# Routed expert rows in grains of 256: two experts' odd grains share one of 20 jobs per half

## What is computed

```python
def _moe_forward(x, Wfc_s, bfc_s, Wproj_s, bproj_s, Wr, Wfc, bfc, Wproj, bproj):
    shared = new_gelu(xf @ Wfc_s + bfc_s) @ Wproj_s + bproj_s        # 128 -> 512 -> 128
    topk_p, topk_i = jax.lax.top_k(jax.nn.softmax(xf @ Wr), 2)
    ...                                                              # gate: the two, normalised
    for e in range(8):
        h = new_gelu(xf @ Wfc[e] + bfc[e]) @ Wproj[e] + bproj[e]
        routed = routed + h * gate[:, e:e + 1]
    return shared + routed
...
x = x + 0.5 * _L0_ffn_ref(_layernorm(x), ...)
x = x + _L0_attn_ref(_layernorm(x), ...)
x = x + 0.5 * _L0_ffn_ref(_layernorm(x), ...)
```

## Time and profile before

| | us |
|---|---|
| median of 3 runs | 1620.02 (1619.47 to 1620.25) |
| the profiled execution's own time | 1619.65 |
| its span, first to last instruction | 1617.8 |
| mean granted clock of TensorE | 0.933 of full |
| PE busy in the span | 87% |
| DVE, ACT, POOL busy | 70%, 63%, 58% |

### The profile page before, as it was taken

The page is one execution under the profiler, slowest core; times in us unless marked ns, Lnnn a source line. Parts: engine busy times, 40 slices in busy tenths (PEclk is TensorE's granted clock), DMA queues, the critical chain, the costliest instruction groups (busy, mean ns, idle before and its releaser), DMA issues.

```text
span 1617.8 us, 31349 instructions
## 1 busy us (share of the span) xinstructions
PE 1414.1 (87%) x10792; PEld 1102.2 (68%) x10792; DVE 1136.0 (70%) x2292; ACT 1017.4 (63%) x1765; POOL 942.4 (58%) x742
## 2 busy tenths in 40 slices
PE   5689899999996799999999999677999999999700
PEld 4668788888884566666666666576877888887500
DVE  7767666667884688888777777576776666788522
ACT  3145478888884477777777777313556888878600
POOL 3168888405661388888565555534877850377176
PEclk9999999999998699999999999758999999999955
DMA  9801256556662646445444443000115655566522
GB/s 264 266 33 42 85 185 201 167 167 192 197 200 91 188 149 174 150 147 170 135 135 142 137 143 106 9 1 23 41 44 189 210 180 157 180 199 199 150 78 74
DMA packets 244702, 226.53 MB, mean 140 GB/s; under 512 B 31809, under 2 KB 188737, under 8 KB 244545
## 3 DMA queue, kind: packets, MB, share of 16 engines
q1 hardware_dynamic: 179584, 166.83, 32.6%
q0 software_dynamic: 16384, 33.59, 7.5%
q10 hardware_dynamic: 48576, 24.12, 5.0%
HBM read 85.34 MB, written 90.70 MB: 109 GB/s over the span
## 4 chain that ended last, share of the span: by engine, by line
PE 40%; issue 9%; POOL 7%; ACT 5%; DVE 4%; DMA 1%; POOLq 0%; DVEq 0%; ACTq 0%; SPq 0%
PE psum L851 5%; POOL x_slots L652 5%; PE psum L832 5%; PE psum L866 3%; PE psum L313 3%; ACT ret_absed L1001 2%; PE psum L315 2%; PE psum L314 2%; PE psum L296 2%; PE psum L295 2%; PE psum L294 2%; PE psum L906 2%; POOL ring L663 2%; PE psum L239 2%; DVE ret_f L1115 1%
## 5 line engine op out<-in xcount | busy, mean ns | idle before, releaser
L663 POOL DMA_INDIRECT ring<-y_slots,slot x256 | 279.1, 1090 | 303.6 <-DMA y_slots<-ffn_y_rows 198.1
L652 POOL DMA_INDIRECT x_slots<-ffn_xn,slot x256 | 323.5, 1263 | 147.5 <-issue 77.4
L598 DVE TENSOR_TENSOR ffn_h_lo<-ffn_h,ffn_h_hi 128x1024 fp32r<-128x1024 f32 x248 | 304.0, 1226 | 8.6
L385 ACT ACTIVATE ffn_h<-psum,ffn_bias_up 128x512 f32<-128x512 f32 x368 | 236.4, 682 | 6.0
L588 DVE TENSOR_TENSOR ffn_x_lo<-psum,ffn_x_hi 128x512 fp32r<-128x512 f32 x124 | 85.8, 692 | 205.6 <-ACT ffn_x_hi L367 205.4
L1261 POOL TENSOR_TENSOR ret_ssum<-ret_ssum,ret_power 128x32 f32<-128x32 f32 x32 | 174.4, 5449 | 42.5 <-DVE ret_ssum L1169 42.3
L1145 DVE TENSOR_TENSOR ret_masked<-psum,ret_mask 128x512 f32<-128x512 f32 x256 | 174.8, 683 | 23.4 <-PE psum L832 18.5
L1001 ACT ACTIVATE ret_absed<-ret_masked 128x1536 f32<-128x1536 f32 x128 | 190.1, 1485 | 1.5 <-PE psum L866 0.4
L596 DVE CAST ffn_h_hi<-ffn_h 128x1024 fp32r<-128x1024 f32 x248 | 171.2, 690 | 7.7 <-PE psum L315 7.5
L995 ACT ACTIVATE ret_masked<-psum 128x256 f32<-128x256 f32 x256 | 96.9, 380 | 105.4 <-DVE ret_masked L1145 105.0
L313 PE MATMUL psum<-ffn_h_hi,ffn_w_down 128*128 128x512 f32 x368 | 152.3, 414 | 5.9 <-issue 5.5
(11 more groups left out here) (155 smaller groups left out, 3059.7 us busy)
## 6 DMA issues: line engine op xcount, KB each, us to landing
qk_copies<-ret_parts SPq DMA_DIRECT2D x128, 256.0 KB
ret_qk<-qk_copies SPq DMA_DIRECT2D x32, 1024.0 KB, 5.6
ffn_xj<-x_slots SPq DMA_DIRECT2D x92, 256.0 KB
ffn_w_up<-w_hi SPq DMA_DIRECT2D x92, 256.0 KB
ffn_w_up<-w_lo SPq DMA_DIRECT2D x92, 256.0 KB
y_slots<-ffn_y_rows ACTq DMA_DIRECT2D x92, 256.0 KB, 3.3
x_slots<-ffn_y_rows SPq DMA_DIRECT2D x46, 256.0 KB, 3.5
x_slots<-ffn_xn,slot POOLq DMA_INDIRECT x256, 2.7
```

Of the source, the lines that this page charges most:

```text
L385: act.activation(h[2 * (n % 2) + c // 2][:, (c % 2) * JOB:(c % 2 + 1) * JOB], up_ps[c % UP_RING], ACT.Gelu_apprx_tanh, bias=bias[:, c:c + ...
L598: dve.tensor_tensor(h_lo[s][:], buf[:], h_hi[s][:].bitcast(F32), ALU.subtract).then_inc(lo_done, 1)
L652: pool.indirect_dma_start(m["x_slot_rows"][half], slots_of(half, k), xn[:, half * HALF + k // 2, :], None)\
L663: pool.indirect_dma_start(ring[:, k % G_RING, :], None, m["y_slot_rows"][half], slots_of(half, k % BLOCKS))\
```

## The change

The unit that an expert's rows are rounded up to is now a grain of 256 rows, `GRAIN`. An expert with an odd number of grains in a half puts its odd grain into a pair job, where it shares 512 rows with the odd grain of another expert; all other grains go in twos into whole jobs, as before. A half has 32 grains and at most 7 more by rounding, so 20 jobs: 4 pair jobs and 16 whole ones. A layer has 16 + 40 = 56 jobs.

- **A pair job** has two weight sets. Its up and down matmuls go by columns 0 to 255 with the first set and 256 to 511 with the second: 24 up and 24 down matmuls of 256 columns. Each gelu and the reading of `y` are split in two (`shares`). `up` waits for both sets before its first matmul.
- **Up weights.** `w_up` still has two buffers, now one per set. SP waits, before set s, for the gelus of the job that used set s-2. A pair uses both buffers.
- **Down weights.** `w_down` has two buffers too; `down_schedule` puts each set's copy at the earliest hidden stage at which its buffer is free. `w_down1` lies over constants that routing alone uses, so the copies wait for `slots_done`.
- **Order.** 13 shared jobs; then pair, shared, pair, shared, pair, shared, pair of the first half; its 16 whole jobs; then the second half, as pair and three whole jobs four times over, and four whole ones.
- **Routing.** `place` on DVE has more steps, 19 more increments of `route` per layer.

```diff
+GRAIN = JOB // 2
-HALF_JOBS = MOST + NE - 1
+PAIR_JOBS = NE // 2
+HALF_JOBS = -(-(TOKENS // GRAIN + NE - 1) // 2)
-SHARED_FIRST = 16
+SHARED_FIRST = 13
...
+    order = shared[:SHARED_FIRST] + pairs[0][:1]
+    for pair, between in zip(pairs[0][1:], shared[SHARED_FIRST:]):
+        order += [between, pair]
+    order += whole[0]
+    for i, pair in enumerate(pairs[1]):
+        order += [pair] + whole[1][3 * i:3 * i + 3]
+    order += whole[1][3 * PAIR_JOBS:]
...
+def down_schedule(jobs):
+    users, slots, last = set_users(jobs), {}, -1
+    for s, (job, i) in sorted(users.items()):
+        free = users[s - 2][0]["n"] + 2 if s >= 2 else 0
+        at = min(max(job["n"], free, last + (i > 0)), job["n"] + 1)
+        assert at >= free
+        slots.setdefault(at, []).append(s)
+        last = at
+    return slots
...
     def place_up(sp, job):
+        for at, s in enumerate(job["sets"]):
+            e = sp.value_load(table[0:1, job["entry"] + at:job["entry"] + at + 1], min_val=1, max_val=NE)
+            if s >= 2:
+                sp.wait_ge(gelu_done, CH * (users[s - 2][0]["n"] + 1))
...
         def up(job):
+            for s in job["sets"]:
+                pe.wait_ge(up_ready[s % 2], up_weights_at(s))
...
+                for cols, parts in zip(shares(job), weights):
+                    bank = up_ps[c % UP_RING][:, cols]
...
+                for cols, added in zip(shares(job), bias):
+                    last = act.activation(to[:, cols], up_ps[c % UP_RING][:, cols], ACT.Gelu_apprx_tanh, bias=added[:, c:c + 1])
...
+            for cols, of in halves_of:
+                dve.tensor_tensor(beyond[:, :, cols], position[:, :, cols], whole_slots[:, of].unsqueeze(2).to_broadcast(wide),
+                                  ALU.is_ge).then_inc(route, 1)
...
+            for cols, of in halves_of:
+                dve.tensor_tensor(beyond[:, :, cols], beyond[:, :, cols], shift[:, of].unsqueeze(2).to_broadcast(wide), ALU.mult)\
+            dve.tensor_tensor(slot_part, slot_part, beyond, ALU.add).then_inc(route, 1)
```

More of the change, by code:

```diff
@@ L67, in job_order @@
-    return jobs
+    pairs, whole = ([[("routed", HALF_JOBS * half + k) for k in ks] for half in range(2)]
+                    for ks in (range(PAIR_JOBS), range(PAIR_JOBS, HALF_JOBS)))
+    order = shared[:SHARED_FIRST] + pairs[0][:1]
[5 more added lines that the diff above has]
+    order += whole[1][3 * PAIR_JOBS:]
+    assert sorted(order) == sorted(shared + pairs[0] + whole[0] + pairs[1] + whole[1])
@@ new lines, in job_order @@
+    jobs, routed_before, shared_before, sets_before = [], 0, 0, 0
+    for layer in range(2):
+        for at, (kind, k) in enumerate(order):
+            routed = kind == "routed"
+            pair = routed and k % HALF_JOBS < PAIR_JOBS
+            sets = range(sets_before, sets_before + (2 if pair else 1 if routed else 0))
+            entry = ENTRIES * (k // HALF_JOBS) + (2 * (k % HALF_JOBS) if pair else k % HALF_JOBS + PAIR_JOBS)
+            jobs.append({"n": len(jobs), "layer": layer, "routed": routed, "k": k, "half": k // HALF_JOBS if routed else None,
+                         "first": at == 0, "last": at == len(order) - 1, "ordinal": routed_before if routed else shared_before,
+                         "pair": pair, "sets": sets, "entry": entry})
+            routed_before += routed
+            shared_before += not routed
+            sets_before += len(sets)
@@ L70, in ffn_programs, with set_users @@
+    return jobs
+def set_users(jobs):
+    return {s: (job, i) for job in jobs for i, s in enumerate(job["sets"])}
+def down_schedule(jobs):
[7 more added lines that the diff above has]
+    return slots
 def ffn_programs(nc, m):
@@ L267, in tensor_route, with shares @@
         place()
+    def shares(job):
+        return [slice(i * GRAIN, (i + 1) * GRAIN) for i in range(2)] if job["pair"] else [slice(0, JOB)]
     def tensor_jobs(pe, layer):
@@ L281, in up @@
             pe.wait_ge(x_lo_done, n + 1)
[L282 to L287, removed]
+            for s in job["sets"]:
+                pe.wait_ge(up_ready[s % 2], up_weights_at(s))
+            weights = [(w_up[s % 2][:, 0, :], w_up[s % 2][:, 1, :]) for s in job["sets"]]\
+                or [(w_hi[:, 0, 0:HID], w_lo[:, 0, 0:HID])]
             for c in range(CH):
@@ L309, in down @@
                     pe.wait_ge(lo_done, 2 * n + c // 2 + 1)
[L310 to L315, removed]
+                for cols, parts in zip(shares(job), weights):
+                    hi, lo = (part[:, c * P:(c + 1) * P] for part in parts)
+                    a_hi, a_lo = (a[c // 2].rearrange("p (c t) -> p c t", c=2)[:, c % 2, cols] for a in (h_hi, h_lo))
+                    pe.matmul(y_ps[:, cols], hi, a_hi, start=(c == 0 and cols.start == 0), stop=False)
+                    pe.matmul(y_ps[:, cols], hi, a_lo, start=False, stop=False)
+                    last = pe.matmul(y_ps[:, cols], lo, a_hi, start=False, stop=(c == CH - 1 and cols.stop == JOB))
                 if c % 2:
@@ L384, in hidden @@
                 act.wait_ge(up_done, CH * n + c + 1)
[L385 to L388, removed]
+                to = h[2 * (n % 2) + c // 2][:, (c % 2) * JOB:(c % 2 + 1) * JOB]
+                for cols, added in zip(shares(job), bias):
+                    last = act.activation(to[:, cols], up_ps[c % UP_RING][:, cols], ACT.Gelu_apprx_tanh, bias=added[:, c:c + 1])
+                last.then_inc(gelu_done, 1)
+                if c == 1:
+                    for s in down_slots.get(n, ()):
+                        if users[s][0]["layer"] == layer:
+                            place_down(s)
         def take_y(job):
@@ L415, in scalar_jobs @@
                 take_y(mine[i - 2])
-            hidden(job, mine[i - 1] if i else None)
+            hidden(job)
             if i + 1 < len(mine):
@@ L423, in scalar_jobs @@
         take_y(mine[-2])
-        if mine[-1]["routed"]:
-            place_down(mine[-1])
+        for s in down_slots.get(mine[-1]["n"] + 1, ()):
+            if users[s][0]["layer"] == layer:
+                place_down(s)
         if mine[-2]["routed"]:
@@ L525, in place @@
-            dve.tensor_tensor(end[:], start[:], jobs_of[:], ALU.add).then_inc(route, 1)
-            dve.tensor_scalar(start_slot[:], start[:], float(JOB), None, ALU.mult).then_inc(route, 1)
-            dve.wait_ge(route, base + 9)
[L528 to L532, removed]
+            for w in range(2):
+                for half in range(2):
+                    dve.tensor_tensor(pairs[:, 2 * w + half], parts_of[:, w, half].unsqueeze(1).to_broadcast([P, NE, NE]), lower,
+                                      ALU.mult).then_inc(route, 1)
```

185 lines of the change are left out of this document (109 added, 76 removed).

## The result

| | before | after |
|---|---|---|
| median, us | 1620.13 (1619.47 to 1621.16) | 1668.84 (1667.41 to 1669.85) |
| ratio | | 1.0299, 95% interval 1.0282 to 1.0317 |
| profiled execution, span | 1619.65, 1617.8 | 1667.87, 1666.0 |
| mean granted clock of PE | 0.933 | 0.899 |

The change made the kernel slower by 48.7 us. The forecast was 51.7 us, in a range of 25 to 78.

What follows compares the result with a forecast made beforehand. PE was taken to bound the steady routed jobs, 6.45 us each. Per layer -19.35 + 3.2 + 29.1 + 2.8 + 1.9 + 1.0 = +18.7, for both +37.3, plus 14.4 for the clock: 1671.8 us, range 1645 to 1698.

Steps and rivals of the forecast that it cites:

- Stalls at the up weights: PE waits for late up weights at or right behind pairs, 9 times per layer: +29.1 us per layer.
- The rival in which the weights are there in time: PE does not stand at the up weights around pairs, so the kernel is faster: 1599.1 us, chance 0.07.
- Landing in 4.6 us: An up weight set's three DMAs: last issue 1.28 us after the first, plus 3.3 us to land; ends 4.0 and 5.6.
- the sum from the rows: Forecast total of 1671.8 us, with the up weights' landing taken from DMA times in the profile rows.
- The clock at half of the stalls: PE's granted clock falls behind half of the 18 up weight stalls, at 1.6 us each: +14.4 us; chance 0.57.
- the rival with a fall at every stall: PE's granted clock falls behind all 18 up weight stalls: 1686.2 us, chance 0.15.
- Three jobs, not six: Of six jobs fewer per layer, three only lengthen PE's wait for the scatter before the first pair: gain 19.35 us, not 38.7.
- The scatter's end: Longer DVE routing starts the scatter 6.6 us later, 3.4 us is won back while DVE stands: +3.2 us per layer.
- Double copies: ACT copies two down weight sets in a row five times per layer, delaying x_hi and x_lo: +2.8 us per layer.
- First pair's second set: The first pair's second up weight set lands about 1 us after PE wants it: +1.0 us per layer.

Runs made afterwards that it cites:

- e1: Changed kernel with a third up weight buffer, so SP waits for the gelus of the job that used set s-3: 1589.71 us.
- e3: Changed kernel without a set's third DMA, the 2 KB bias (loaded only for the first two sets of a layer): 1655.63 us.
- e2: Changed kernel with 11 extra 512-column matmuls into an unused bank ahead of the up weight wait at 18 places: 1653.18 us.
- e5: e1 with all 16 shared jobs first and the pairs of both halves spaced by three whole jobs: 1567.27 us.
- e6: e5 with the second of two down weight sets that ACT copies in a row put behind x_hi of the next job: 1559.47 us.
- e4: Kernel before, with SP waiting for the gelus of the job right ahead at 9 of 46 routed jobs per layer, no pairs: 1681.40 us.

## Why the prediction was right, by its own steps

- **Stalls at the up weights, forecast 58.2 us and 14.4 for the clock.** Right in place, number and cause: nine per layer, at each pair of the second half and behind each pair that a whole job follows. The idle time of these 18 is 51.7 us, and e1 puts the price of stalls and clock together at 79.1 us, where the two terms gave 72.6. The split between the two kinds was off: the ones ahead of a pair were 3.0 to 4.6 us, 3.4 in the mean (forecast 2.9), those behind one 1.5 to 3.4 us, 2.4 in the mean (forecast 3.5). Where the pair had run at half clock the wait behind it was shorter, but it was 2.8 us even behind a pair at full clock. The rival in which the weights are there in time needed them 2.5 us after the first issue; the fastest took 4.3.
- **Landing in 4.6 us.** 4.3 to 5.8 us from SP's first issue to PE's start, 4.6 in the mean of the 18. Its form, last issue plus a landing, is borne out by e3. The Trainium skill, DMA: Bandwidth & Descriptors, section Anatomy of one DMA — SWDGE (gpsimd) path, gave an estimate of 3.8 us from the first issue until the weights are there, and with it 1657 us. The 4.3 to 5.8 us above are longer than that, and the measured 1668.8 us lies nearer to the sum from the rows.
- **The clock at half of the stalls.** It fell at 15 of the 18, not at 9. Its price, 15.7 us net by e2 against 14.4, came out right by offset, which is luck: more falls, but part of each taken up by the next wait. So the rival with a fall at every stall (1686.2 us) is refuted in its price, and nearly right in its count. The Trainium skill, TensorE: Matmul & The Clock Gate, section HAM oscillation — how this bites in real kernels, tells of a kernel that ran slow after each of its waits. The traces here come close to that, with 15 of 18, but a fall cost less in time than the half speed alone would say: 15.7 us net against 33.
- **Three jobs, not six.** Right: the idle time ahead of the first pair went from 5.90 to 19.63 us (forecast 22), and e5 got 22.4 us of the other three jobs' 38.7 back.
- **The scatter's end, forecast +3.2 us.** This is the term that was mis-sized: +0.9 us in the first layer. The instructions that were added on tiny tiles (14, not 13) took 0.20 us each and not the 0.29 that I had taken as their mean, so the scatter started 5.5 us later and not 6.6, and it won back 4.5 us instead of 3.4 while the other engines stood. In the second layer the time from its start to the first row load is 98.3 us against 102.1 before, so 3.8 won back there.
- **Double copies, 5.5 us for ten.** e6 gives roughly 0.49 us each, 4.9.
- **First pair's second set, 2.0 us.** The wait was 0.32 us in the first layer and 0.40 in the second; the turn and down matmuls ahead of it ran in part at half clock (0.68 from 196.3 to 202.3 us) and covered more.
- Without stalls and clock I had -20.9 us left; e1 has 1589.7 - 1620.4 = -30.7. In the traces of before and e1 the 9.8 us lie as follows. The first layer's row load starts 0.4 us later than before, where 3.2 was forecast: 2.8 us. From the first row load to the last down matmul the layers take 15.1 and 16.6 us less than before, where -19.35 + 2.8 + 1.9 + 1.0 = -13.65 was forecast for each: 4.4 us, of which the second set and the copies explain some 2. The remaining 2.6 us stay open. This surplus and the 6.5 us too few on stalls and clock cancel, which is luck and why the sum is nearer than its terms.

## What to carry to other kernels

Before work is packed more tightly, count what a tighter job holds of each ring: a job that takes two slots of a ring of two turns a load ahead of time into a load on the path, and a set's DMAs need 4.3 to 5.8 us for that here. A wait on the same buffer one job closer costs, each time, what is left of that landing when PE wants the weights (1.1 to 3.4 us in e4), and at many of them the clock behind it; one more buffer, in space that is free in that phase, was worth 79 us. And a job that is left out only counts behind the last thing that gates the stage: ask for each what starts next, and what that is waiting for.

## What the runs showed of the hardware

- The granted clock of PE fell to 0.50 behind idle times much shorter than the 5 us that the kernel before shows. In the kernel before it had stayed up behind 1.55 us; in e3 it fell behind 1.79 us in the first layer, and stayed up behind another 1.79 us in the second. The timeline of PE in e3 shows the end of the first:

```profile
370.33 0.47 PE L339 MATMUL psum<-ffn_x_hi,ffn_w_up 128*128 128x512 f32 x1 [1.79 <-issue]
```

and the windows view of PE, 1.2 us later, the clock:

```profile
371.50:374.50 3.00, 3.00 (x8) 0.50 0.93 288
```

- The length of one idle time alone does not decide: in the changed kernel it stayed at 1.00 behind 2.96 us and fell behind the next one of 2.82 us (the windows from 361.70 and 371.30 above). These are the two starts, with the first matmul at full and at half speed:

```profile
361.70 0.36 PE L338 MATMUL psum<-ffn_x_hi,ffn_w_up 128*128 128x256 f32 x1 [2.96 <-DMA ffn_bias_up<-biases]
...
371.31 0.76 PE L338 MATMUL psum<-ffn_x_hi,ffn_w_up 128*128 128x512 f32 x1 [2.82 <-issue]
```

- POOL's indirect scatters took 1.23 us each while PE, ACT and DVE stood (the changed kernel) and 1.57 us each beside all three at work (e5), for the same tiles. Which of the three slows them, or whether it is the traffic of their DMAs, no run here parts. Leaving them without work so gave back 4.5 us of the scatter for which they waited.
